# Attention block of a decoder layer: the sums of exponents are made in the values pass itself, and five engines take their work in a new order

## The reference, cut to what matters

```python
# end of block 1: out is what the recurrence left
out = (out - mu) * rsqrt(var + EPS) * gamma + beta
out = (out * silu(x @ Wg)) @ Wout
x1 = layernorm(x + out)
# block 2, for each sequence
Q, K, V = proj(x1, Wq, bq), proj(ctx, Wk, bk), proj(ctx, Wv, bv)
scores = einsum('bhqd,bhkd->bhqk', Q, K) / 4
attn = softmax(scores, axis=-1)
out = einsum('bhqk,bhkd->bhqd', attn, V) @ Wo.T + bo
x2 = layernorm(x1 + out)
```

## Time and profile before

| what | value |
|---|---|
| median of three runs | 2107.28 us (2105.57 to 2107.8) |
| profiled execution, own time | 2109.26 us |
| its span, first to last instruction | 2107.3 us |
| mean granted clock of TensorE | 0.98 of full speed |
| busy: PE, DVE, ACT, POOL | 93%, 74%, 59%, 15% of the span |
| first instructions of the attention block | 757.6 us |
| steps of its steady part | one each 23.2 us |

### The profile page before, as it was taken

How to read it: one execution, slowest core, us unless ns; L and a number is a source line. 1 busy time by engine, 2 the same in 40 slices (tenths; PEclk the granted TensorE clock), 3 DMA queues, 4 the chain that set the end, 5 groups by cost and what they waited for, 6 DMA issues and landing times. The chain is left out here.

```text
span 2107.3 us, 72273 instructions
## 1 busy us (share of the span) xinstructions
PE 1955.1 (93%) x29175; PEld 1332.4 (63%) x29175; DVE 1559.2 (74%) x2809; ACT 1236.8 (59%) x2015; POOL 314.9 (15%) x324
## 2 busy tenths in 40 slices
PE   7999999999999879999999999999879988799798
PEld 4666666666666657777777777777634433244687
DVE  6777777777777757767776777677546599998897
ACT  4454444454444436676667667766545666588565
POOL 1111211210100111111111111111100123200022
PEclk9999999999999989999999999999989999999999
DMA  3010010010010011010011001100069788689574
GB/s 121 23 33 24 23 34 23 23 31 26 23 31 26 16 54 32 31 45 30 30 30 45 30 30 39 36 30 30 2 180 276 256 314 312 226 352 425 188 263 157
DMA packets 121319, 205.19 MB, mean 97 GB/s; under 512 B 44851, under 2 KB 98358, under 8 KB 121142
## 3 DMA queue, kind: packets, MB, share of 16 engines
q1 hardware_dynamic: 121142, 202.43, 28.2%
HBM read 108.01 MB, written 85.98 MB: 92 GB/s over the span
## 5 line engine op out<-in xcount | busy, mean ns | idle before, releaser
L1348 PE MATMUL ff_twin<-ff_xq,w_uh 128*128 (+1 forms) x1152 | 347.0, 383 | 39.5 <-DVE ff_top L1717 25.2
L1348 PEld LDWEIGHTS ff_twin<-ff_xq,w_uh 128*128 128x128 f16 x1152 | 110.8, 98 | 189.0 <-issue 44.0
L1348 PE MATMUL ff_twin<-ff_xq,w_ul 128*128 (+1 forms) x576 | 220.1, 382 | 0.0
L545 ACT ACTIVATE x<-rec_e,rec_hidden 128x512 f32<-128x512 f32 x256 | 155.8, 702 | 36.6 <-PE rec_e L380 36.6
L1126 DVE TENSOR_REDUCE mneg<-att_s 128x4 f32<-128x512 f32 x256 | 159.0, 683 | 18.2 <-PE att_s L902 17.2
L661 DVE TENSOR_TENSOR x<-rec_x,rec_until 128x512 f32<-128x512 f32 x256 | 158.8, 682 | 17.5 <-PE rec_x L364 17.5
L392 PE MATMUL rec_x<-x 32*32 32x64 f32 x8192 | 147.2, 219 | 16.4 <-DVE x L661 11.3
L392 PEld LDWEIGHTS rec_x<-x 32*32 32x32 f32 x8192 | 125.9, 107 | 53.4 <-issue 53.0
L1030 ACT ACTIVATE att_e<-att_s 128x512 f32<-128x512 f32 x256 | 132.2, 604 | 36.5 <-PE att_s L922 36.5
L349 PE MATMUL rec_f<-rec_xT,w_rec 128*128 128x256 f32 x512 | 137.9, 403 | 0.9 <-ACT rec_v L527 0.9
L341 PE MATMUL rec_f<-w_rec,rec_xT 128*128 128x512 f32 x256 | 128.5, 625 | 6.2 <-DVEq L594 5.0
(11 more groups left out here) (245 smaller groups left out, 4359.2 us busy)
## 6 DMA issues: line engine op xcount, KB each, us to landing
raw_scratch<-ff_out SPq DMA_DIRECT2D x32, 768.0 KB, 3.5
ff_in<-raw_scratch SPq DMA_DIRECT2D x32, 768.0 KB, 5.9
gate_scratch<-ff_out SPq DMA_DIRECT2D x28, 768.0 KB, 3.6
ff_in<-gate_scratch SPq DMA_DIRECT2D x28, 768.0 KB, 9.2
product_scratch<-ff_out SPq DMA_DIRECT2D x28, 768.0 KB, 8.8
ff_out<-product_scratch SPq DMA_DIRECT2D x28, 768.0 KB, 5.9
att_x<-in_x SPq DMA_DIRECT2D x32, 256.0 KB, 2.7
att_ctx<-in_ctx SPq DMA_DIRECT2D x32, 256.0 KB, 2.9
```

The lines of the kernel that those rows point to most:

```text
L545: A.activation(out, E[(s + k) % 2][:], ACT.Exp, bias=hidden[:, asks, r:r + 1] if r < NR else 0.0, scale=-1.0 if asks else 1.0).then_inc(q[ ...
L1348: m = T.matmul(bank_.rearrange("p (b n) -> p b n", b=BT), weights(wp, kc, a, c), tile[:, xp, :, kc], start=(i == 0), stop=(i == len(terms) ...
```

## The change

The values matrix is filled with ones where it had zeros (the memset at the end of the recurrence), so that one matmul of 32 columns gives the 16 features of a head and, in the other 16 partitions, its sum of exponents. Even and odd heads have sums and features the other way round, and each now has 128 columns of its own in the bank. DEN goes. ACT takes Ln of both halves with a scale and bias by partition (0 and 1 where there are features, which gives a log of zero), POOL adds the two, ACT takes Exp of minus the sum; DVE shuffles the partitions so that each factor stands at its features (`att`), brings the features together with a predicated copy inside the bank (`merge`), and multiplies.

Each engine's `step` is written anew around a step number with pairs at -3 to +2 of it (`older`, `old`, `prev`, `now`, `next_`, `after`): the front of pair now+1 up to its output matmul, keys, values, x1 and queries of pair now, the attention of pair now-1, and the ends of pair now-2. The attention table loads go from three in a step to two. SP's loads and their wait stay.

```diff
-                G.memset(t["v_half"][:], 0.0).then_inc(qw["cleared"], 1)
+                G.memset(t["v_half"][:], 1.0).then_inc(qw["cleared"], 1)
...
+        VO = BA.rearrange("p (o k q) -> p k o q", o=KC, k=2)
+        CROSS = [HD + i for i in range(HD)] + list(range(HD))
...
+            for p in range(-2, 4):
+                step(near(0, p))
+            with eng.Fori(2, (NP - 2) // 2) as j:
+                for u in range(2):
+                    step(near(j, u))
+            for p in range(NP - 2, NP + 3):
+                step(near(0, p))
...
                 def values(p, b):
...
-                            T.matmul(DEN[rows(j)].rearrange("p (o q) -> p o q", o=KC), t["ones_half"][:, k],
-                                         e[:, b, j].rearrange("p (o m q) -> p m o q", o=KC, m=2)[:, k],
-                                         start=(k == 0), stop=False, skip_group_check=True)
...
+                    for c in range(4):
                         for j in range(NR):
+                            m = T.matmul(BA[rows(j), c * P:(c + 1) * P],
+                                         t["v_half"][:, p.s, b, 4 * (c // 2) + j, c % 2 * 2 * HD:(c % 2 + 1) * 2 * HD],
+                                         e[:, b, j, c * P:(c + 1) * P], start=True, stop=True)
                     m.then_inc(q["pv_made"], 1)
...
+                def step(at):                                          # PE
+                    old, prev, now, next_ = at(-2), at(-1), at(0), at(1)
+                    if old:
+                        att_out(old, 0)
+                    if now:
+                        keys(now)
+                    if prev:
+                        scores(prev, 0)
+                    if old:
+                        values(old, 1)
+                    if next_:
+                        turn_o(next_)
+                        turn_x(next_)
+                    if now:
+                        vals(now)
+                    if prev:
+                        turn_maxima(prev, 0)
+                        again(prev, 0)
+                        shift(prev, 0)
+                    if old:
+                        att_out(old, 1)
+                    if next_:
+                        turn_context(next_)
+                    if now:
+                        turn_x1(now)
+                    if prev:
+                        scores(prev, 1)
+                        values(prev, 0)
+                    if next_:
+                        gate(next_)
+                    if now:
+                        query1(now)
+                    if prev:
+                        turn_maxima(prev, 1)
+                        again(prev, 1)
+                        shift(prev, 1)
+                    if now:
+                        query0(now)
+                    if next_:
+                        out(next_)
...
+                def logs(p, b):
+                    n = 2 * p.r + b
                     act.wait_ge(q["pv_made"], n + 1)
+                    wait_if(act, q["crossed"], n)
+                    for k in range(2):
+                        A.activation(ld[:, k], VO[:, k], ACT.Ln, bias=t["part"][:, k:k + 1],
+                                     scale=t["part"][:, 1 - k:2 - k]).then_inc(q["ld_ready"], 1)
+                def inverse(p, b):
+                    act.wait_ge(q["ls_ready"], 2 * p.r + b + 1)
+                    A.activation(rc, ld[:, 0].rearrange("p o q -> p (o q)"), ACT.Exp, scale=-1.0).then_inc(q["rc_ready"], 1)
...
+                def step(at):                                          # ACT
+                    old, prev, now, next_ = at(-2), at(-1), at(0), at(1)
+                    if old:
+                        exps(old, 1)
+                    if now:
+                        keys_out(now)
+                    if prev:
+                        A.preload_act_table_set("natural_log_exp_and_others")
+                    if old:
+                        logs(old, 1)
+                    if next_:
+                        x_out(next_)
+                    if old:
+                        inverse(old, 1)
+                    if next_:
+                        o_out(next_)
+                    if prev:
+                        shift_out(prev, 0)
+                        exps(prev, 0)
+                    if now:
+                        x1_out(now)
+                    if prev:
+                        logs(prev, 0)
+                    if next_:
+                        context_out(next_)
                         A.preload_act_table_set("exp_and_others")
+                        gate_out(next_)
+                    if prev:
+                        shift_out(prev, 1)
+                        inverse(prev, 0)
+                    if now:
+                        query_out(now)
...
+                def merge(p, b):
+                    dve.wait_ge(q["ld_ready"], 2 * (2 * p.r + b) + 2)
+                    V.copy_predicated(VO[:, 0], t["part"][:, 1:2].bitcast(mybir.dt.int32).unsqueeze(2).to_broadcast([P, KC, P]),
+                                      VO[:, 1]).then_inc(q["merged"], 1)
+                def att(p, b):
...
+                    V.stream_shuffle(sw.rearrange("p o q -> p (o q)"), rc, CROSS).then_inc(q["crossed"], 1)
...
+                    V.tensor_tensor(attT[:], VO[:, 0], sw[:], ALU.mult).then_inc(q["att_ready"], 1)
...
+                def step(at):                                          # DVE
+                    older, old, prev, now, next_, after = at(-3), at(-2), at(-1), at(0), at(1), at(2)
+                    # residual_1(now), residual(old, 0), stats_1(now), apply_o(next_), maxima(prev, 0),
+                    # merge(old, 1), att(old, 1), vals_out(now), apply_1(now), apply2(older, 1),
+                    # residual(old, 1), stats2(old, 0), maxima(prev, 1), merge(prev, 0), stats2(old, 1),
+                    # gated(next_), att(prev, 0), apply2(old, 0), stats_o(after)
...
+                def both(p, b):                                        # POOL
+                    pool.wait_ge(q["ld_ready"], 2 * (2 * p.r + b) + 2)
+                    G.tensor_tensor(ld[:, 0], ld[:, 0], ld[:, 1], ALU.add).then_inc(q["ls_ready"], 1)
...
+                    # power var_o(next_), both(old, 1), power var_1(now), power var_2(older, 1),
+                    # biased(now), both(prev, 0), power var_2(old, 0)
```

More of the change, by code:

```diff
@@ L877, in across @@
                     m.then_inc(done, 1)
[L879 to L884, removed]
                 def along(bank_, lhs, wt, done):
@@ new lines, in x1_out, with o_out @@
+                def x1_out(p):
+                    act.wait_ge(q["x1T_made"], p.r + 1)
+                    A.activation(flat(x1T), F[0][:], ACT.Copy).then_inc(q["x1T_ready"], 1)
+                def o_out(p):
+                    act.wait_ge(q["onT_made"], p.r + 1)
+                    wait_if(act, q["y_ready"], p.r)
+                    for kc in range(KC):
+                        A.activation(ogb[:, kc], F[2][:, kc * 2 * P:(kc + 1) * 2 * P], ACT.Identity,
+                                     bias=t["beta"][:, kc:kc + 1], scale=t["gamma"][:, kc:kc + 1]).then_inc(q["ogb_ready"], 1)
@@ new lines, in step @@
+                def step(at):
+                    older, old, prev, now, next_, after = at(-3), at(-2), at(-1), at(0), at(1), at(2)
+                    if now:
+                        residual_1(now)
+                    if old:
+                        residual(old, 0)
+                    if now:
+                        stats_1(now)
+                    if next_:
+                        apply_o(next_)
+                    if prev:
+                        maxima(prev, 0)
+                    if old:
+                        merge(old, 1)
+                        att(old, 1)
+                    if now:
+                        vals_out(now)
+                        apply_1(now)
+                    if older:
+                        apply2(older, 1)
+                    if old:
+                        residual(old, 1)
+                        stats2(old, 0)
+                    if prev:
+                        maxima(prev, 1)
+                        merge(prev, 0)
+                    if old:
+                        stats2(old, 1)
+                    if next_:
+                        gated(next_)
+                    if prev:
+                        att(prev, 0)
+                    if old:
+                        apply2(old, 0)
+                    if after:
+                        stats_o(after)
@@ new lines, in step @@
+                def step(at):
+                    older, old, prev, now, next_ = at(-3), at(-2), at(-1), at(0), at(1)
+                    if next_:
+                        power(q["var_o"], next_.r + 1, mv_o[:, :, 1], rs_o[:], q["rstd_o"])
+                    if old:
+                        both(old, 1)
+                    if now:
+                        power(q["var_1"], now.r + 1, mv_1[:, :, 1], rs_1[:], q["rstd_1"])
+                    if older:
```

(7 more changed lines are left out.)

422 lines of the change are left out of this document (182 added, 240 removed).

## The result

The changed kernel takes 2027.66 us (2024.32 to 2032.23) against 2107.54 on the same chip: a ratio of 0.962 (95% interval 0.9608 to 0.9633), 80 us less.

A forecast was written before the change was run, and what follows sets the result against it. PE bounds the kernel: its step of 23.2 us falls to a floor of 20.8, plus 0.6 for near ties is 21.4. 779.3 + 16 + 30 x 21.4 + 35 = 1472.3, 59 less, gave 2049 us, range 2034 to 2080.

The forecast's parts named there:

- PE is the bound, and DEN's time lies on its path: Attention steps: only PE has no room, so dropping two DEN stages of 0.89 saves 1.78 us per step.
- The floor of 20.8: PE's least time per attention step: 23.2 less 1.78 for DEN, 0.3 of waits and 0.3 for fewer shape changes.
- the changes of shape: PE's switches between full, 32-row and 32-column matmuls: 15 become 10 per step, worth 0 to 0.8 us, taken as 0.3.
- 0.6 for near ties: Added per step to PE's floor because ACT's and DVE's chains all lie within 0.3 us of PE.
- place 1: From the end of keys to the first shift: ACT needs 6.1 us in PE's 6.4, slack 0.3.
- place 2: From the end of the first values to the second shift: ACT 4.0 us against PE's 4.1; gate's products end 0.1 before out.
- DVE second by a hair: DVE's work with its own waits takes 20.2 to 20.7 us per step, beside PE's 20.8.
- Prices of the new instructions: Taken per instruction: Ln with scale and bias 0.56 us, predicated copy 0.45, shuffle 0.45, POOL's add 0.75.
- A table load without a drain behind it: On ACT, the Ln starts 1.30 us after its load's start, without the skill's further drain of 1380 ns.
- Start and end: First x1b at 779.3 us as before, the second 16 later, and 35 from the last to the next block.
- the rival below it: PE's floor is reached and shape changes pay in full: step 20.6 us, 2025 to 2034, chance 0.07.
- The slower rivals: A predicated copy in PSUM of over 1.9 us makes DVE slow the kernel; at 2.3 us 2132; chance 0.05.

The follow-up runs named there:

- e1: The changed kernel with DEN's eight matmuls per item put back on PE in front of the values: step 21.98 us against 20.36, median 2080.2 us.
- e2: The changed kernel with the transpose of the maxima again between the halves of the second scores: step 20.68 us against 20.36, median 2039.7 us.
- e9: The old order with the new sums, x1T and the context copied out between ACT's logs and its Exp: step 24.50 us, median 2149.7 us.
- e5: The changed kernel with two more table loads on ACT between keys and shift: step 23.90 us against 20.36, median 2134.7 us.
- e4: The changed kernel with one more reduction on DVE ahead of each item's maxima: step 20.89 us with 0.6 per item, 20.58 with 0.4, against 20.36.
- e7: The changed kernel with five spare matmuls on PE in the waits of the start: 2024.7 us against 2027.6 on the same chip.
- e8: The changed kernel with spare matmuls on PE in the start and in the waits of the last three steps: 2021.4 us against 2027.6 on the same chip.
- e6: The kernel before, in its old order, with only the new way to the sums: step 25.30 us against 23.23, median 2177.0 us.
- e3: The changed kernel with scores and values no longer side by side on PE, transposes moved between them: step 21.74 us against 20.36, median 2072.7 us.

## Why the prediction was wrong, by its own steps

*PE is the bound, and DEN's time lies on its path*: right. It was worth 1.62 per step (e1) and not 1.78.

*The floor of 20.8*: this is the step that failed. It came from 23.2 less 1.78, less 0.3 of waits, less 0.3 for the changes of shape. The changed kernel's step is 20.36 with 0.57 of waits in it (the table below), so what PE has to do in it is 19.8. The floor was 1.0 too high, 30 us over the 30 steps, and two of its terms were mis-sized.

The first is the changes of shape: 0.16 each (e2), 0.8 for five, at the very top of the 0 to 0.8 that the prediction had written down, and taken as 0.3. The Trainium skill (TensorEngine Tiling (Array Packing), Key Properties) says that changing the tiling mode drains TensorE; the trace agrees in so far as each change costs 0.16 with nothing to wait for, but doesn't show what that time is made of.

The second is the waits: 0.3 was what the windows show as PE idle, and the waits inside stages, which the rows count as busy, were put at nothing. They can be estimated by comparing each stage, from start to start, with the shortest time that the same stage takes between the same kinds of neighbours in any of the traces. These are means over the steps between 900 and 1380 us:

| stage | before | its shortest | changed | its shortest |
|---|---|---|---|---|
| both queries | 2.06 | 1.73, as the keys | 1.93 | 1.83, in e2 |
| transposes of o | 0.80 | 0.53, as those of x1 in the changed kernel | 0.49 | 0.49 |
| both shifts | 0.81 | 0.66, in e2 | 0.79 | 0.66 |
| both scores | 2.33 | 2.21, in e9 | 2.44 | 2.21 |
| second scores, first halves | 1.35 | 1.29, in e2 | not split | |
| output matmul | 1.92 | 1.92, in e9 | 1.83 | 1.73, in e2 |
| waits in a step | 0.92 | | 0.57 | |

The kernel before, in the stages with the largest of these waits; the queries are 1318.28 to 1320.34:

```profile
1313.38 0.60 PE L867 MATMUL att_f<-ident,att_on 128*128 128x128 f32 x4
1314.18 1.07 PE L932 MATMUL att_a<-att_e,ones_half 128*32 128x256 f32 x16 [0.20 <-ACT att_e L1030]
...
1316.55 1.89 PE L875 MATMUL att_f<-att_cT,w_x 128*128 128x256 f32 x8
1318.28 2.22 PE L882 MATMUL att_f<-att_x1T,w_x 128*128 128x256 f32 x8
```

With these two terms the sum closes: 23.2 less 1.78 for DEN, less 0.8 for the shapes, less 0.9 of old waits, plus 0.57 of new ones is 20.3, against 20.36 measured. No run took the waits of the old order away by themselves, so their 0.9 rests on this comparison and on the closed sum. The new order alone, with DEN's work still on PE, is 1.25 faster (e1 against before): 0.8 of that is shape, and the rest is waits, 0.92 in the kernel before and 0.47 in e1 by the same comparison.

*0.6 for near ties*: 0.57 was measured, but no row stood behind the 0.6, so its size is luck. Two of its three places are where the walk had put them. The shifts wait 0.13 per step for ACT (place 1, slack 0.3 in the walk), and `query0` and the output matmul together 0.20, as the gate's products come late from DVE (place 2, slack 0.1). The third is one that the walk left out: the second item's scores stand 0.24 per step until ACT's last exponential of the first item has cleared its bank. In e5, where PE comes later, the same scores take 1.10 and not 1.34. The changed kernel's own waits over 200 us, which name two of these:

```profile
PEld att_f L901 <- DVE att_yT L1312: 3.2, 10, 0.4
...
PEld att_s L1011 <- ACT mT L1124: 1.4, 8, 0.2
```

*DVE second by a hair*: right as far as e4 shows, at an estimated 19.7 to 19.9 where 20.2 to 20.7 was said.

*Prices of the new instructions*: right, within 0.03. *A table load without a drain behind it*: right. In e5 three loads follow each other 1.28 to 1.29 apart, and the logs start 1.30 after the last one.

*Start and end*: 7 us too early for the first `x1b` and 7 too short for the end. The walk had the chain in front of the first `x1b` unchanged. In the new order PE has little to do before the first tanh, and the granted clock is 0.53 from 769 to 779 us: 3.75 for a stage of 1.97. In the kernel before the keys run ahead of that gate, and the clock is 1.00 in the same 10 us. e7 shows the clock's part by taking it away, about 4 us. The other 3 lie behind the output matmul: from its start to the first `x1b` it is 9.2 in e7 and 5.7 before, as DVE now copies the values out, for which it waits 2.98, ahead of the normalization that gives x1. At the end the clock is a part too: it is 0.71 there and 1.00 in e8, whose end is 1.4 to 4.4 shorter.

*The range* had 2034 as its lower end, with a chance of 0.07 for the rival below it (period 20.6, 2025 to 2034). The measured time lies in that rival, and half of its condition is what happened: the shape changes pay in full. The other half is not: PE's floor was not reached but was itself lower, by waits of the old order that no rival had. The prediction's words that the range takes in the upper half of this case don't fit its numbers, as the case ends where the range begins.

*The slower rivals*: none came true in this order. But e6 shows that the same new instructions are 65 us slower than before in the old one. The forecast priced DEN's time as if any order kept it; the 2.9 per step need both halves. Old order, old sums 23.23; old order, new sums 25.30; new order with new sums and DEN's work 21.98; new order, new sums 20.36.

*What would show it*: every sign came as said but the spacing (values 1.01, loads 64, Ln 0.56, PE 100%, DVE 90), and none of the three signs of being wrong did. All of them looked for a step that is longer than forecast; none could have shown a floor that is too high.

## What to carry to other kernels

A saving on the engine that is the bound counts only if the work that replaces it finds a place in the queues of the others: in its old order, this kernel became slower by it, in part because an urgent copy stood behind ACT's new work. A busy share of 99 or 100% does not say that an engine never waits. Before taking a period less its idle time as a floor, compare each stage, from start to start, with the shortest that the same stage takes elsewhere in the traces. And when an experiment adds work to a step with waits in it, read the price from the rows at the place itself: the step's growth shows only what no wait absorbed. An idle stretch on TensorE costs more than its length when the granted clock falls behind it; matmuls that do nothing, in waits that can't be removed, bring it back.

## What the runs showed of the hardware that was not expected

- A wait of 1.54 us of PE, repeated in each step of a busy loop, was followed by 3.2 us at a granted clock of 0.58, so that 2.57 us of added loads cost 3.54 per step (e5). Waits of up to 0.70 in e3 left it at 1.00.
- A switch between full and 32-row matmuls costs 0.16 us (e2: 0.32 for the two of each item, from start to start); the step grew by only 0.32 for four, as waits took the rest.
- PE rows showed 100.00 busy of 100 us in the changed kernel, in steps of 20.36 with 0.57 of waits inside them.
- A predicated copy of 128x256 float32 inside PSUM, with a mask broadcast from SBUF, takes 0.428 us, a shuffle of the same size 0.438, and a plain product 0.424 (changed kernel).
- Spare matmuls in the start held the granted clock at 1.00 where it was 0.53, and brought the first `x1b` 3.6 to 4.3 us earlier, counted from the block's first instruction on DVE (e7).
